# A mixture-of-experts stage in a fused two-layer block: biases, router and first matmuls rearranged

## The chip, the cores and the metric

The kernel runs on one core of one Trainium2 chip. The metric is the device time of one execution in microseconds (us); lower is better. Engines: PE is TensorE, DVE VectorE, ACT ScalarE, POOL GpSimd, SP SyncE, which here only issues DMAs.

## What is computed

Two layers over 2048 tokens of width 128 (8 sequences of 256). Layer 0 is an adaptive layer norm with causal attention (16 heads of 8), a second adaptive layer norm, and a feed-forward of nine experts: eight chosen by a router (two for each token, weights renormalised) and one shared. Layer 1 is a gated recurrence with a small MLP and a second mixture of eight experts. The change touches the feed-forward of layer 0:

```python
def _ffn(x, w1, b1, w2, b2):
    h = jax.nn.gelu(x @ w1.T + b1)
    return h @ w2.T + b2
logits = xf @ router_w.T + router_b
routing = softmax(logits)
sel_w, sel_idx = top_k(routing, 2)
sel_w = sel_w / sel_w.sum(-1)
comb[token, sel_idx] = sel_w
out = _ffn(xf, shared...) + sum_e comb[:, e] * _ffn(xf, spec_e...)
```

## The kernel before, in words

Activations lie transposed: 128 features on the partitions, tokens along the free axis, in four blocks of 512 tokens (t = 0 to 3). X is the residual stream, HN the normalised input. Matrix products keep fp32 precision by splitting each operand into a rounded upper part and a rest (HH and HL of the input, WH and WL of the weights, GH and GL of the hidden layer) and adding three matmuls (`three`, lines 1125 to 1129).

Each engine has its own instruction list, written out by hand in the order of execution, with waits on semaphores between them. The list around the change, in the order of the program:

The **end of attention** (lines 854 to 916 on VectorE, 1285 to 1350 on TensorE): units of one head group at a time, then the out projection (`out_proj`, four matmuls of 512 columns), and the second layer norm, called norm 1: `mean`, `centre`, `square`, `variance`, `inverse` (Ln and Exp on ScalarE), `normalise`, `split_hidden` (GpSimd, HH) and `rest` (VectorE, HL). Blocks 0 to 2 of it run early; block 3 comes last, since it waits for the last sequence's attention.

The **router** (`router`, line 1156; `route`, line 699): 16 tiny matmuls make logits in PSUM for all tokens. VectorE adds the router's bias, takes a maximum and subtracts it, ScalarE takes one Exp (`router_exp`), and 15 small VectorE instructions, each waiting for the one before, find the largest and the second largest (a tie goes to the lower expert), and divide. COMB then has a share for each token and expert, with 1 for the shared one. TensorE transposes it (`route_out`), VectorE copies the nine rows to CT (line 923), SyncE stores them in memory and loads each row back, repeated on all 128 partitions, as WB (lines 224 to 234).

The **experts**, one step for each of 36 pairs m of expert and block. TensorE computes four hidden chunks of 128 (`hidden0`, chunk c of step m+1) alternating with four output chunks of step m (`output0`). ScalarE takes Gelu twice from PSUM, into G and rounded into GH (lines 508 and 509); VectorE subtracts (`lower0`, line 937) to give GL; `output0` waits for GL. VectorE multiplies the finished output by WB (`moe_scale`, line 756), and GpSimd adds it to ACC (line 312) and splits the weights two experts ahead (lines 289 and 292). One step has 24 matmuls of 512 columns on TensorE.

How the first steps differ: `lower0` of step 0 is done by GpSimd (line 349), which splits expert 1's weights after it. ACC starts as the sum of the output biases: four matmuls of B2 with CT in full fp32 (`bias_out`, line 1361, one after each output chunk of step 1) and four VectorE copies (`bias_sum`, line 928).

## Time and profile before

| what | value |
|---|---|
| median of 3 runs | 679.75 us (679.01 to 680.6) |
| the profiled execution | 679.79 us, of which the span from first to last instruction is 678.0 us |
| PE, DVE, ACT, POOL busy | 606.8, 545.4, 486.1, 173.3 us |
| mean granted TensorE clock | 0.949 of 2.4 GHz |
| the chain that ended last, by engine | PE 62%, DVE 26%, ACT 5%, issue 5% |
| the expert stage of layer 0 | from about 214 to 430 us of the span |

Busy shares are means over stages that are bound by different things. What a change in one stage is worth is read from that stage: which engine is never idle there, and for what the others wait. The chain that ended last follows the work back from the last instruction. The granted clock is 1.00 at 2.4 GHz and 0.50 at 1.2 GHz.

### The profile page before, as it was taken

Reading aid. Unit: us, or ns where it says so; the run is one execution under the profiler, and the core shown is the slowest. Engines: PE = TensorE matmul, PEld = TensorE weight load, DVE = VectorE, ACT = ScalarE, POOL = GpSimd, SP = SyncE. Lnnn points to the kernel's source line nnn. Section 1 sums busy time; section 2 is a strip of 40 time slices with the busy share of each in tenths; the row PEclk is TensorE's granted clock in tenths of the full one; section 3 lists DMA queues with packets and bytes.
Section 4 is the critical chain, followed back from the end, with each engine's and each line's share of the span. In section 5 each row is a group of like instructions: output and inputs, shape, how many; then the busy total and the mean of one; then the engine's idle time right before and its main releaser. Section 6 shows DMA issues by size and latency. Waiting matters only on the chain.

```text
span 678.0 us, 11084 instructions
## 1 busy us (share of the span) xinstructions
PE 606.8 (89%) x3284; PEld 441.1 (65%) x3284; DVE 545.4 (80%) x1345; ACT 486.1 (72%) x857; POOL 173.3 (26%) x147
## 2 busy tenths in 40 slices
PE   8788889888997899999999999782699899999996
PEld 5355556555545568888888887351385788888884
DVE  3667888888866658878888887756899689999997
ACT  4548999999553669999999998677635466666663
POOL 3422223332301415443554443310143000000000
PEclk9789999999996899999999999976699799999999
DMA  7000000000100120122202220000000042222201
GB/s 239 1 0 2 2 2 0 0 0 0 32 1 0 48 113 37 57 95 94 91 2 93 93 85 1 23 1 0 0 1 0 1 150 87 87 86 86 86 1 62
DMA packets 6651, 29.85 MB, mean 44 GB/s; under 512 B 887, under 2 KB 1024, under 8 KB 4417
## 3 DMA queue, kind: packets, MB, share of 16 engines
q1 hardware_dynamic: 6610, 29.37, 12.2%
q8 instruction: 18, 0.29, 0.2%
q14 instruction: 23, 0.19, 0.1%
HBM read 28.18 MB, written 1.19 MB: 43 GB/s over the span
## 4 chain that ended last, share of the span: by engine, by line
PE 62%; DVE 26%; issue 5%; ACT 5%; DMA 1%; SPq 0%; POOL 0%; DVEq 0%; ACTq 0%; POOLq 0%
PE PS L1127 16%; PE PS L1129 16%; PE PS L1128 16%; DVE STAT L802 8%; PE PS L1273 2%; DVE RA L822 2%; PE PS L1228 2%; DVE HN L656 2%; PE PS L1153 2%; DMA AR<-in_wmod 1%; DVE SU L828 1%; PE PS L1242 1%; DVE HN L652 1%; ACT RA L605 1%; DVE AR L1086 1%
## 5 line engine op out<-in xcount | busy, mean ns | idle before, releaser
L937 DVE TENSOR_TENSOR RA<-AR,RA 128x512 fp32r<-128x512 f32 x140 | 134.3, 983 | 29.1 <-ACT RA L509 28.4
L508 ACT ACTIVATE AR<-PS,BI 128x512 f32<-128x512 f32 x144 | 99.4, 691 | 26.2 <-PE PS L1129 16.6
L1127 PE MATMUL PS<-HH,WH 128*128 128x512 f32 x272 | 109.5, 403 | 0.1
L1129 PE MATMUL PS<-HL,WH 128*128 128x512 f32 x272 | 107.4, 395 | 0.0
L1128 PE MATMUL PS<-HH,WL 128*128 128x512 f32 x272 | 107.3, 395 | 0.0
L509 ACT ACTIVATE RA<-PS,BI 128x512 fp32r<-128x512 f32 x144 | 98.4, 683 | 0.0
L802 DVE CUSTOM_DVE_ANT_0 STAT<-PS,MQ 128x128 f32<-128x128 f32 (+1 forms) x256 | 76.3, 354 | 20.2 <-PE PS L1229 20.1
L1127 PE MATMUL PS<-RA,WH 128*128 128x512 f32 x208 | 82.4, 396 | 2.5 <-DVE RA L1093 2.1
L1129 PE MATMUL PS<-RA,WH 128*128 128x512 f32 x208 | 81.2, 391 | 0.0
L1128 PE MATMUL PS<-RA,WL 128*128 128x512 f32 x208 | 81.2, 390 | 0.0
L312 POOL TENSOR_TENSOR AR<-AR 128x512 f32<-128x512 f32 x32 | 51.2, 1601 | 111.9 <-DVE AR L756 111.9
L335 POOL TENSOR_TENSOR RA<-QKT,RA 128x512 fp32r<-128x512 f32 x32 | 40.8, 1275 | 110.5 <-ACT RA L437 107.5
L605 ACT ACTIVATE RA<-AR 128x512 fp32r<-128x512 f32 x64 | 40.4, 632 | 34.2 <-DVE AR L1086 33.3
L1127 PEld LDWEIGHTS PS<-HH,WH 128*128 128x128 f32 x272 | 52.2, 192 | 15.6 <-ACT RA L509 3.0
L1129 PEld LDWEIGHTS PS<-HL,WH 128*128 128x128 f32 x272 | 51.9, 191 | 11.1
L1128 PEld LDWEIGHTS PS<-HH,WL 128*128 128x128 f32 x272 | 52.2, 192 | 10.7 <-issue 0.2
L444 ACT ACTIVATE AR<-PS 128x768 f32<-128x768 f32 x64 | 48.4, 808 | 13.7 <-PE PS L1246 11.6
L1153 PE MATMUL PS<-STAT,OND 128*128 128x512 f32 x48 | 31.5, 762 | 22.6 <-ACT STAT L386 22.6
L1093 DVE TENSOR_TENSOR RA<-AR,RA 128x512 fp32r<-128x512 f32 x64 | 44.3, 691 | 7.5 <-ACT RA L605 2.7
L599 ACT ACTIVATE AR<-PS 128x512 f32<-128x512 f32 x64 | 38.2, 597 | 13.8 <-PE PS L1129 11.8
L1127 PEld LDWEIGHTS PS<-RA,WH 128*128 128x128 f32 x208 | 39.2, 188 | 12.5 <-DVE RA L1093 3.2
L1086 DVE TENSOR_TENSOR AR<-AR 128x512 f32<-128x512 f32 x64 | 43.8, 685 | 2.2 <-ACT AR L614 2.2
(196 smaller groups left out, 1185.1 us busy)
## 6 DMA issues: line engine op xcount, KB each, us to landing
AR<-comb SPq DMA_DIRECT2D x16, 1024.0 KB, 4.6
WS<-in_w SPq DMA_DIRECT2D x9, 512.0 KB, 5.6
WS<-in_w SPq DMA_DIRECT2D x8, 384.0 KB, 3.1
M<-in_mats SPq DMA_DIRECT2D x1, 1384.0 KB, 12.2
X<-in_xT SPq DMA_DIRECT2D x4, 256.0 KB, 4.8
out_xT<-X SPq DMA_DIRECT2D x4, 256.0 KB, 2.1
AR<-in_wmod SPq DMA_DIRECT2D x1, 768.0 KB, 9.2
KM<-in_kmats SPq DMA_DIRECT2D x1, 162.5 KB
```

The source lines that it names most:

```text
L312: gp.tensor_tensor(out=blk(ACC, t), in0=blk(ACC, t), in1=YW[:, t % 2, :], op=ALU.add)\
L444: act.activation(PR[:, n0 % 2, 2 * h:2 * h + 2, :], PS[:, 2 + 2 * h:4 + 2 * h, 0:384], ACT.Exp, scale=SCALE).then_inc(exp_done, 1)
L508: act.activation(G[:, c, :], PS[:, c, :], ACT.Gelu_apprx_tanh, bias=bias).then_inc(s["act"], 1)
L509: act.activation(GH[:, m0 % 2, c, :], PS[:, c, :], ACT.Gelu_apprx_tanh, bias=bias)\
L605: act.activation(GH[:, m % 2, c, :], G[:, c, :], ACT.Copy).then_inc(s1["gh"], 1)
L802: mm = dve.tensor_tensor_reduce(out=MASKED_S[:, q, j, 0:width], in0=PS[:, j, first:first + width], in1=MQ[:, 256 - width:256], scale=-1.0, ...
L937: dve.tensor_tensor(out=GL[:, m0 % 2, c, :], in0=G[:, c, :], in1=f(GH[:, m0 % 2, c, :]), op=ALU.subtract).then_inc(s["lo"], 1)
L1086: dve.tensor_tensor(out=G[:, c, :], in0=G[:, c, :], in1=WB[:, e % 2, t * BLK:(t + 1) * BLK], op=ALU.mult).then_inc(s1["ymul"], 1)
L1127: pe.matmul(out, wh, xh, start=first, stop=False)
L1128: pe.matmul(out, wl, xh, start=False, stop=False)
L1129: return pe.matmul(out, wh, xl, start=False, stop=last)
L1153: pe.matmul(PS[:, variance_bank(k, t), :], OND[:, :], blk(STAT, t), start=True, stop=True)\
```

## The change

Five edits in the feed-forward of layer 0. The output biases are no longer summed by matmuls: a column `b2` for each expert joins the vectors, `moe_scale` adds it in the same VectorE instruction that multiplies by WB, and GpSimd fills ACC with the shared expert's bias. The routing no longer needs the softmax: two are chosen from the logits, and the shares are (1 ± tanh((second − first)/2))/2, the tanh being a ScalarE instruction between two Gelus. The small routing instructions stand between those of `lower0` of step 0, which VectorE now does. The hidden chunks of step 0 stand ahead of the last block's variance and normalisation on TensorE, and expert 1's weights are split ahead of the norm on GpSimd. The transposes stand in step 1 where they stood in step 0, and the VectorE loop over 24 steps is written out.

GpSimd:

```diff
             gp.wait_ge(moe[0]["w_in"], 16)
             split_weights(0, 0, 0, 1024)
+            gp.wait_ge(moe[0]["w_in"], 32)
+            split_weights(0, 1, 1, 1024)
             for t in range(NBLK):
                 split_hidden(1, HN, t)
-            for c in range(4):
-                gp.wait_ge(moe[0]["act"], 2 * (c + 1))
-                gp.tensor_tensor(out=GL[:, 0, c, :], in0=G[:, c, :], in1=f(GH[:, 0, c, :]), op=ALU.subtract)\
-                  .then_inc(moe[0]["lo"], 1)
-            gp.wait_ge(moe[0]["w_in"], 32)
-            split_weights(0, 1, 1, 1024)
+            gp.wait_ge(wo_done, 4)
+            shared_bias = V[:, VAT["b2"] + E0 - 1:VAT["b2"] + E0]
+            gp.tensor_scalar(ACC, shared_bias.to_broadcast([128, TOK]), 1.0, 0.0, ALU.mult, ALU.add)\
+              .then_inc(moe[0]["acc_init"], 1)
```

ScalarE:

```diff
-            router_exp(0)
...
+            def router_tanh():
+                act.wait_ge(s["odds"], 1)
+                act.activation(ODDS[:, :], RM["den"][:, :], ACT.Tanh, scale=0.5).then_inc(s["exps"], 1)
...
-            for m in range(8):
+            gelus(0, 0, 0)
+            gelus(1, 1, 0, between=router_tanh)
+            for m in range(2, 8):
                 gelus(m, m, m // 4)
```

VectorE, first `moe_scale`, then the list:

```diff
-                dve.tensor_tensor(out=YW[:, m0 % 2, :], in0=PS[:, 4 + m0 % 4, :],
-                                  in1=WB[:, slot, t * BLK:(t + 1) * BLK], op=ALU.mult).then_inc(s["ymul"], 1)
+                dve.scalar_tensor_tensor(out=YW[:, m0 % 2, :], in0=PS[:, 4 + m0 % 4, :], scalar=bias,
+                                         in1=WB[:, slot, t * BLK:(t + 1) * BLK], op0=ALU.add, op1=ALU.mult)\
+                   .then_inc(s["ymul"], 1)
...
+            centre(1, 3)
             rest(1, HN, 0)
             rest(1, HN, 1)
-            centre(1, 3)
             rest(1, HN, 2)
             normalise(1, 3)
             rest(1, HN, 3)
-            route(0, E0)
...
-            dve.wait_ge(s["lo"], 4)
-            lower0(1, 1)
-            for t in range(NBLK):
-                bias_sum(t)
+            lower0(0, 0, (largest, first_equal, second_largest, second_chosen))
+            shares()
+            lower0(1, 1, (nothing, nothing, first_rows_in, last_rows_in))
             lower0(2, 2)
```

TensorE:

```diff
             router(0, 0)
             router(0, 1)
             mean(1, 3)
             router(0, 2)
+            pe.wait_ge(s["split"], 2)
+            hidden0(0, 0, 0)
+            hidden0(0, 0, 1)
             variance(1, 3)
+            hidden0(0, 0, 2)
+            hidden0(0, 0, 3)
             router(0, 3)
...
-            for c in range(4):
-                hidden0(0, 0, c)
-            step0(0, 0, 1, between=routes_between)
-            step0(1, 1, 1, between=biases_between)
+            step0(0, 0, 1)
+            step0(1, 1, 1, between=routes_between)
```

`largest`, `first_equal`, `second_largest`, `second_chosen` and `shares` hold 2, 3, 5, 3 and 5 small instructions. `first_rows_in` and `last_rows_in` are the copies of line 923, two each.

The first place is TensorE's list from the last block's mean (`X,OND`) to the first expert matmul. M,HN is a router matmul, STAT,OND the variance, HH and HL with WH and WL a hidden chunk. Before:

```order
L1140 MATMUL PS<-X,OND 128x512 [waits x_upd]
L1161 MATMUL PS<-M,HN 128x8 [waits hn_done]
L1161 MATMUL PS<-M,HN 128x8 x3
L1153 MATMUL PS<-STAT,OND 128x512 [waits lnv_done,sq_done]
L1161 MATMUL PS<-M,HN 128x8 [waits hn_done]
L1161 MATMUL PS<-M,HN 128x8 x3
L1127 MATMUL PS<-HH,WH 128x512 [waits moe0_split,hl_done]
```

Now:

```order
L1195 MATMUL PS<-X,OND 128x512 [waits x_upd]
L1216 MATMUL PS<-M,HN 128x8 [waits hn_done]
L1216 MATMUL PS<-M,HN 128x8 x3
L1182 MATMUL PS<-HH,WH 128x512 [waits cen_done,hl_done,moe0_split]
L1183 MATMUL PS<-HH,WL 128x512
L1184 MATMUL PS<-HL,WH 128x512
L1182 MATMUL PS<-HH,WH 128x512 [waits cen_done,hl_done]
...
L1208 MATMUL PS<-STAT,OND 128x512 [waits lnv_done,sq_done]
L1182 MATMUL PS<-HH,WH 128x512 [waits cen_done,hl_done]
...
L1216 MATMUL PS<-M,HN 128x8 [waits hn_done]
```

Two hidden chunks now stand ahead of the last variance and two behind it, and the last router matmuls follow them.

The second place is VectorE's list from the last `rest` to the second subtraction of step 1 (RA<-AR,RA is `lower0`). Now:

```order
L675 TENSOR_TENSOR HL<-HN,HH 128x512 [waits hh_done]
L751 MEMSET COMB 128x16
L754 TENSOR_TENSOR AR<-PS,ROWS 128x128 [waits moe0_logits,in_rows]
L757 TENSOR_REDUCE RM_m<-AR 128x16 [waits moe0_rstep]
L1001 TENSOR_TENSOR RA<-AR,RA 128x512 [waits moe0_act]
L762 TENSOR_TENSOR AR<-AR,RM_m 128x128 [waits moe0_rstep]
...
L797 TENSOR_TENSOR AR<-AR,ODDS 128x128 [waits moe0_exps,moe0_rstep]
L799 TENSOR_TENSOR AR<-AR 128x128 [waits moe0_rstep]
L801 TENSOR_SCALAR COMB<-AR 128x16x8 [waits moe0_rstep]
L1001 TENSOR_TENSOR RA<-AR,RA 128x512 [waits moe0_act] x2
L981 COPY AR<-PS 9x512 [waits moe0_combT] x2
```

Before, all the routing (19 instructions) and its four copies stood ahead of the first subtraction on this engine.

The third place is GpSimd's list around the hidden split. Before:

```order
L289 TENSOR_SCALAR WH<-WS 128x1024 [waits moe0_w_in]
L292 TENSOR_TENSOR WL<-WS,WH 128x1024 [waits moe0_split]
L300 TENSOR_SCALAR HH<-HN 128x512 [waits hn_done] x4
L349 TENSOR_TENSOR RA<-AR,RA 128x512 [waits moe0_act] x4
```

Now:

```order
L291 TENSOR_TENSOR WL<-WS,WH 128x1024 [waits moe0_split]
L288 TENSOR_SCALAR WH<-WS 128x1024 [waits moe0_w_in]
...
L299 TENSOR_SCALAR HH<-HN 128x512 [waits hn_done] x4
L350 TENSOR_SCALAR AR<-V 128x2048 [waits wo_done]
```

The second weight split stands ahead of the hidden split, and the fill of ACC (2048 columns) directly behind its last block.

## Rows read from the trace of the kernel before

**Rows 1.** Stretches: us, PE, PEld, DVE, ACT, POOL busy (count), PE clock, DMA.

```profile
215.00:220.00 5.00, 5.00 (x14) 4.05 (x15) 3.73 (x13) 3.15 (x6) 0.12 (x1) 0.50 0.00 0
...
300.00:400.00 100.00, 100.00 (x443) 82.84 (x442) 86.06 (x93) 92.93 (x153) 50.46 (x29) 1.00 0.18 64
```

**Rows 2.** The chain that ended last, 190 to 262 us: start, us, what.

```profile
215.78 0.30 DVE AR L721
...
230.25 0.92 PE PS L1174 x8
...
233.91 1.05 PE PS L1366 x2
...
244.24 0.50 PE PS L1127
```

**Rows 3.** The timeline, end of the norm to the first Gelu: start, us, engine.

```profile
206.68 1.28 DVE L668 TENSOR_TENSOR HL<-HN,HH 128x512 fp32r<-128x512 f32 x2
...
209.28 1.65 PE L1153 MATMUL PS<-STAT,OND 128*128 128x512 f32 x2 [1.40 <-ACT STAT L386]
210.97 0.69 ACT L392 ACTIVATE STAT<-PS,CON 128x512 f32<-128x512 f32 x1 [1.74 <-PE PS L1153]
...
213.08 0.73 DVE L656 TENSOR_SCALAR HN<-HN,MC,MOD 128x256 f32<-128x256 f32 x2
...
214.55 0.69 DVE L668 TENSOR_TENSOR HL<-HN,HH 128x512 fp32r<-128x512 f32 x1 [0.74 <-POOL HH L300]
...
217.24 1.28 ACT L508 ACT_TABLE_LOAD   x1
```

**Rows 4.** The timeline, routing on VectorE beside GpSimd.

```profile
219.88 5.16 POOL L349 TENSOR_TENSOR RA<-AR,RA 128x512 fp32r<-128x512 f32 x4 [5.37 <-ACT RA L509]
...
220.02 0.29 DVE L738 TENSOR_REDUCE RM_km<-AR 128x16 f32<-128x128 f32 x1
...
220.34 0.98 DVE L739 TENSOR_TENSOR AR<-AR,RM_km 128x128 f32<-128x128 f32 x1
...
225.01 1.04 POOL L289 TENSOR_SCALAR WH<-WS 128x1024 fp32r<-128x1024 f32 x1
```

**Rows 5.** The timeline near the end of attention.

```profile
175.80 2.35 POOL L292 TENSOR_TENSOR WL<-WS,WH 128x1024 fp32r<-128x1024 f32 x1
175.86 2.32 DVE L815 TENSOR_TENSOR MP<-NM,MP 128x8 f32<-128x8 f32 x1
...
178.18 0.33 SPq L223 DMA_DIRECT2D WS<-in_w  x1
...
183.77 0.17 DVE L815 TENSOR_TENSOR MP<-NM,MP 128x8 f32<-128x8 f32 x1
...
184.23 0.43 DVE L828 STREAM_SHUFFLE SU<-OT 128x256 f32<-128x256 f32 x1
...
186.11 0.42 DVE L822 TENSOR_TENSOR RA<-RA,PS 128x256 fp32r<-128x256 f32 x1 [1.44 <-PE PS L1282]
```

**Rows 6.** DMA issues between 170 and 200 us, with us to landing.

```profile
WS<-in_w SPq DMA_DIRECT2D x1, 512.0 KB, 4.6
```

**Rows 7.** Groups, 260 to 420 us: line, count | busy, mean ns | idle before, releaser.

```profile
L937 DVE TENSOR_TENSOR RA<-AR,RA 128x512 fp32r<-128x512 f32 x118 | 119.1, 1033 | 24.7 <-ACT RA L509 24.1
```

**Rows 8.** Views of single lines: ns min/median/max, first and last start.

```profile
L756 DVE TENSOR_TENSOR AR<-PS,AR x32: 676/683/684, 250.6 to 419.2; 128x512 f32<-128x512 f32 x32
...
L1031 DVE SCALAR_TENSOR_TENSOR AR<-PS,V,AR x12: 735/743/750, 490.7 to 509.4; 128x512 f32<-128x512 f32 x12
```

**Rows 9.** The gates' way through memory: issues, landing, first use.

```profile
232.08 0.31 SPq L225 DMA_DIRECT2D comb<-AR  x1
234.53 0.82 SPq L228 DMA_DIRECT2D AR<-comb  x2
...
DMA to landing us min/median/max: 4.3/4.5/6.5
...
250.56 0.68 DVE L756 TENSOR_TENSOR AR<-PS,AR 128x512 f32<-128x512 f32 x1
```

More of the change, by code:

```diff
@@ L30, with build @@
 MAT_AT, MN = columns(MATS)
[L33 removed]
+def build(nc, xT, wmod, vecs, mats, kmats, rows, w0, w1, comb0, comb1, outT):
     f32, r32, bf16 = mybir.dt.float32, mybir.dt.float32r, mybir.dt.bfloat16
@@ L510, in gelus @@
                        .then_inc(s["act"], 1)
+                    if between and c == 1:
+                        between()
                     if m0 % 4 == 3 and c == 0 and m0 < 35:
@@ new lines, in _, with each, route1, link @@
+            lg, e, k1, k2, e2, w = (RT[k][:, :, :] for k in ("lg", "e", "k1", "k2", "e2", "w"))
+            peak, m1, km1, m2, km2, den = (RM[k][:, :] for k in ("m", "m1", "km1", "m2", "km2", "den"))
+            prio = V[:, VAT["prio"]:VAT["prio"] + 8].unsqueeze(1).to_broadcast([128, 16, 8])
+            logits = PS[:, 7, 0:128].rearrange("p (i e) -> p i e", e=8)
+            def each(x):
+                return x.unsqueeze(2).to_broadcast([128, 16, 8])
+            def route1():
+                s = moe[1]
+                count = [0]
+                def link(ins):
+                    count[0] += 1
+                    ins.then_inc(s["rstep"], 1)
+                    dve.wait_ge(s["rstep"], count[0])
+                dve.wait_ge(s["logits"], 1)
+                dve.tensor_copy(lg, logits).then_inc(s["lg"], 1)
@@ L744, in route, with largest @@
                 dve.tensor_tensor(out=COMB[:, :, 0:8], in0=w, in1=each(den), op=ALU.mult).then_inc(s["comb"], 1)
-                if ne == 9:
-                    dve.memset(COMB[:, :, 8:9], 1.0).then_inc(s["comb"], 1)
-            def moe_scale(s, m, m0, pair):
+            def largest():
+                s = moe[0]
+                dve.memset(COMB[:, :, 8:9], 1.0).then_inc(s["comb"], 1)
+                dve.wait_ge(in_rows, 16)
+                dve.wait_ge(s["logits"], 1)
+                dve.tensor_tensor(out=lg, in0=logits, in1=ROWS[:, 128:136].unsqueeze(1).to_broadcast([128, 16, 8]),
+                                  op=ALU.add).then_inc(s["rstep"], 1)
+                dve.wait_ge(s["rstep"], 1)
+                dve.tensor_reduce(m1, lg, axis=AX.X, op=ALU.max).then_inc(s["rstep"], 1)
@@ new lines, in first_equal, with second_largest @@
+            def first_equal():
+                s = moe[0]
+                dve.wait_ge(s["rstep"], 2)
+                dve.tensor_tensor(out=k1, in0=lg, in1=each(m1), op=ALU.is_equal).then_inc(s["rstep"], 1)
+                dve.wait_ge(s["rstep"], 3)
+                dve.tensor_tensor(out=k1, in0=k1, in1=prio, op=ALU.mult).then_inc(s["rstep"], 1)
+                dve.wait_ge(s["rstep"], 4)
+                dve.tensor_reduce(km1, k1, axis=AX.X, op=ALU.max).then_inc(s["rstep"], 1)
+            def second_largest():
+                s = moe[0]
+                dve.wait_ge(s["rstep"], 5)
+                dve.tensor_tensor(out=k1, in0=k1, in1=each(km1), op=ALU.is_equal).then_inc(s["rstep"], 1)
+                dve.wait_ge(s["rstep"], 6)
+                dve.scalar_tensor_tensor(out=e2, in0=k1, scalar=-3e38, in1=lg, op0=ALU.mult, op1=ALU.add)\
+                   .then_inc(s["rstep"], 1)
+                dve.wait_ge(s["rstep"], 7)
+                dve.tensor_reduce(m2, e2, axis=AX.X, op=ALU.max).then_inc(s["rstep"], 1)
+                dve.wait_ge(s["rstep"], 8)
+                dve.tensor_tensor(out=den, in0=m2, in1=m1, op=ALU.subtract).then_inc(s["odds"], 1)
+                dve.tensor_tensor(out=k2, in0=e2, in1=each(m2), op=ALU.is_equal).then_inc(s["rstep"], 1)
@@ new lines, in second_chosen, with shares @@
+            def second_chosen():
+                s = moe[0]
+                dve.wait_ge(s["rstep"], 9)
+                dve.tensor_tensor(out=k2, in0=k2, in1=prio, op=ALU.mult).then_inc(s["rstep"], 1)
+                dve.wait_ge(s["rstep"], 10)
+                dve.tensor_reduce(km2, k2, axis=AX.X, op=ALU.max).then_inc(s["rstep"], 1)
+                dve.wait_ge(s["rstep"], 11)
+                dve.tensor_tensor(out=k2, in0=k2, in1=each(km2), op=ALU.is_equal).then_inc(s["rstep"], 1)
+            def shares():
+                s = moe[0]
+                dve.wait_ge(s["rstep"], 12)
+                dve.tensor_tensor(out=e, in0=k2, in1=k1, op=ALU.subtract).then_inc(s["rstep"], 1)
+                dve.tensor_tensor(out=w, in0=k1, in1=k2, op=ALU.add).then_inc(s["rstep"], 1)
+                dve.wait_ge(s["rstep"], 14)
+                dve.wait_ge(s["exps"], 1)
+                dve.tensor_tensor(out=e, in0=e, in1=each(ODDS[:, :]), op=ALU.mult).then_inc(s["rstep"], 1)
+                dve.wait_ge(s["rstep"], 15)
+                dve.tensor_tensor(out=w, in0=w, in1=e, op=ALU.add).then_inc(s["rstep"], 1)
+                dve.wait_ge(s["rstep"], 16)
+                dve.tensor_scalar(COMB[:, :, 0:8], w, 0.5, None, ALU.mult).then_inc(s["comb"], 1)
@@ L750, in moe_scale @@
+            def moe_scale(s, m, m0):
+                bias = V[:, VAT["b2"] + m // 4:VAT["b2"] + m // 4 + 1]
+                pair = m // 8
                 slot = m0 // 4 % 2
```

107 lines of the change are left out of this document (39 added, 68 removed).

## The prediction

> **What bounds the kernel now.** I read the stretches first. From 300 to 400 us, in the middle of the expert stage, TensorE is busy all the time at the full clock, 443 matmuls in 100 us, 0.226 us each, so a step of 24 takes 5.44 us; ScalarE's 153 instructions take 0.61 us each and leave it free for 7% of the time [rows 1]. VectorE has idle time there too: 24.7 us ahead of 118 subtractions, 0.84 us for each step of four [rows 7]. So nothing off TensorE can speed up the middle, and what can be won lies in the opening. From 215 to 220 us the clock is at its lower level, 1.2 GHz [rows 1]. Then the chain that ended last: the logits are ready at 215.78, and only at 244.24 does TensorE take up step 2 and is never idle again until the stage ends [rows 2]. Between lie 48 matmuls of steps 0 and 1 and 12 of the first hidden chunks; at 0.226 us all 60 are 13.6 us of work in 28.5 us. The chain there goes through routing on VectorE, transposes and four full-precision bias matmuls of 1.05 us each [rows 2]. The timeline gives the norm ahead of it [rows 3], and shows VectorE held up by GpSimd in two places [rows 4, 5]. The mark to follow is **the start of step 2**, 244.24 us: whatever it gains, the kernel gains, since the stage behind it is bound by TensorE.
>
> **The change part by part.** All times are those of the profiled execution, 679.79 us with a span of 678.0; the median of the three runs, 679.75, is the same to 0.04.
>
> *End of attention, +0.95 us.* The split of expert 1's weights moves here, and its load is issued at 178.18 [rows 5] and lands 4.6 us later [rows 6], at 182.8. GpSimd then rounds for 1.04 us [rows 4] and subtracts for 2.35, which for expert 0 held a VectorE instruction of 0.17 us for 2.32 [rows 5]. The same instruction (line 815) comes next at 183.77, when the rounding is about to end (183.85). I expect the subtraction to hold it until 186.3. Behind it stand a divide and a shuffle, over 0.73 us after its own end [rows 5], so line 822, for which TensorE waits, starts at 187.05 in place of 186.11. Bounds: 0, if the hold misses it; 2.3, the whole hold on the path. I take 0.95, by the rows' own times. TensorE's out projection covers the rest of the hold.
>
> *The norm of block 3, -0.4 us.* On VectorE `centre` now precedes the three `rest` of 0.64 us [rows 3]. First `rest` done: 206.7 + 0.65 + 0.65 = 208.1, when TensorE takes the first hidden chunk, where it was idle before. Two chunks, 6 x 0.226 = 1.36, then the variance at 209.5. It took 1.65 us until 210.97 at the lower clock [rows 3]; two passes of that size take 1.05 at the upper one [rows 2], which I expect, as TensorE is no longer idle just before. So ScalarE reads it at 210.57 and the norm ends at 213.4 instead of 213.81 [rows 3]. The other two hidden chunks fill a stretch in which TensorE was idle. Bound: +0.8 with the low clock. The order of `centre` and `rest` and the early wait for the split (long done at 186.3) cost nothing.
>
> *The first subtraction, -2.9 us.* It ended at 221.2 on GpSimd (219.88 plus a quarter of 5.16) [rows 4]. Now: logits 1.95 us after the norm as before (213.81 to 215.78 [rows 2, 3]), at 215.35. GpSimd's HH of block 3 is ready 0.74 us after the norm [rows 3], at 214.15, and the fill of ACC follows at once. The trace has no such fill; 1024 columns took 1.04 us [rows 4], so 2048 take about 2.1, to 216.2. Its input is one column read over and over. Whether that holds VectorE is not shown. The upper bound is the whole 2.1 us: beside GpSimd's subtraction, a routing instruction with two operands in SBUF took 0.98 in place of 0.29, while a one-operand reduce kept its 0.29 [rows 4]. The lower bound is 0. I take the whole hold, as the `rest` of block 3, also with two such operands, is released at the very moment: it runs from 216.2 to 216.9, the two instructions of `largest` at a pitch of 0.32 [rows 4] to 217.5, the subtraction of 0.69 to 218.2. Without the hold the logits decide: 215.35 + 0.64 + 0.69 = 216.7.
>
> The Trainium skill (SBUF — State Buffer, Who interferes with whom) says that a VectorE instruction with two SBUF inputs contends with a GpSimd one that reads SBUF, not with one that only writes. By it the fill, which reads its column, would hold, and the result is the 669.1 below; counted as a mere write it would be 667.6.
>
> ScalarE is no limit: the Exp is gone, and the table load of 1.28 us [rows 3] moves behind the norm's last Exp (about 211.9), so Gelus run from 213.5, two of them 1.3 us by the mean of rows 1, far ahead of 217.5.
>
> *From there to step 2.* VectorE: 3, 5 and 3 small instructions between subtractions, then 5 for the shares, 16 x 0.32 = 5.1; three more subtractions of step 0 and the first of step 1, 4 x 0.65 = 2.6. That is 7.7 us. TensorE then still has four output and three hidden chunks of 0.68 and 2 x 0.92 of transposes [rows 2]: 6.6. Together 14.35. TensorE's own work from the first output chunk on is 45 matmuls and the transposes, 10.2 + 1.8 = 12.0; I expect the low clock for its first 4 us, as after idle time in rows 1, which adds 2: also 14. So step 2 starts at 218.2 + 14.3 = 232.5, and the opening gains 244.24 - 232.5 = **11.7 us**. The copies, 0.65 each, and the bias matmuls and copies that are gone, 4 x 1.05 on TensorE, lie within this count. The tanh is a small instruction ready before its Gelu is.
>
> *The middle, 0.* `moe_scale` becomes a three-operand instruction; one with the same operands (line 1031) has 743 ns, `moe_scale` 683 [rows 8]. 0.06 us a step against 0.84 idle: hidden. If that idle time were gone, 32 steps would cost 2. At the stage's end, where VectorE finishes, one is on the path: +0.1 with rounding. The written-out loop adds no instruction and I cost it at 0.
>
> *The gates.* The last copy ended at about 232.0, the store was issued at 232.08, the first row's load at 234.53, landing in 4.5 us (4.3 to 6.5), about 7 after the store; the first use was at 250.56, 6.3 after step 2's start [rows 2, 9]. Now the copies end at about 230.7, so the gates land near 237.7 to 239.7 and are wanted at 238.8: late by 0.9 at most. Queued behind the scale is the next step's subtraction, which TensorE wants a step (5.44 us) later, so this costs nothing. It was covered by 11 us before, and is not now.
>
> Sum: 0.95 - 11.7 + 0.1 = -10.65, and 679.79 - 10.65 = **669.1 us**.
>
> **The rivals.**
> 1. *Neither hold bites.* The fill lets VectorE through and the split misses line 815. 1.5 and 0.95 less: 666.7. For it: the fill has a one-column input, and a landing 0.3 us off changes who is first. Against it: both holds are in the trace [rows 4, 5].
> 2. *The clock stays low through the opening.* The 45 matmuls at 0.45 us and slower transposes make 23.1 us of the 14.3, and the time 677.9; a clock that comes back 6 us later than I take costs 3, 672.1. For it: TensorE still pauses three times between the hidden chunks and the first output. Against it: once TensorE was kept busy before, the clock rose in the opening itself, and the two transposes-of-eight at 0.92 are at the upper level [rows 2].
> 3. *The gates come late.* Beyond about 4 us of lateness VectorE, and so TensorE, waits. With the longest landing, 6.5, and the next weights ahead of it, 1 to 2 us: 670.6.
> 4. *VectorE becomes the bound and the kernel is slower.* The place is `moe_scale`, if its third operand made it wait for GpSimd. It decides from 0.84 - 0.06 + 10.65/32 = 1.1 us more a step. If it waited for one whole GpSimd subtraction of 5.16/4 = 1.29 [rows 4] and the next expert's rounding of 1.04 each time, 2.3 a step, 32 x (2.3 - 0.78) = 49 less 10.65 gives 718; at 1.29 alone, 32 x 0.51 = 16 less 10.65, **685.4**. Against it: the present one never took more than 684 ns, the three-operand one never over 750 [rows 8].
> 5. *The change doesn't do what it says: a second table load.* Two loads of 1.28 us around the tanh, one of them hidden: 670.4. The changed instruction list has none there. The Trainium skill (ScalarE: Activation LUTs, Table sets: the hidden batching unit) lists tanh with exp and with sigmoid, not with gelu, by which such loads would be needed.
>
> **How the numbers follow.** My forecast has 0.62 and its own range, 667.6 to 671, from the bounds of fill, split and clock; rival 1 has 0.18, rival 2 0.09, rival 3 0.06, rival 4 0.04, rival 5 0.01. The range 666.2 to 672.1 takes in rivals 1, 3, 5 and the milder half of 2. A measurement of this kernel tells about 0.2%, 1.4 us, from no change. Faster by more: all but rival 4 and the end of rival 2, 0.95; within: 0.01; slower 0.04.
>
> **What would show it.** Step 2 starts near 233.5 (232.5 and the 0.95) instead of 244.2. Line 815's second-last instance lasts over 2 us. The fill takes about 2.1 us, and the `rest` of block 3 or the first subtraction ends late by it. The steps from 260 to 400 stay at 5.44 us with TensorE always busy. The scale's mean is near 743 ns. No table load stands between the first Gelu and the end of the stage. The prediction is wrong if step 2 starts outside 230 to 237, or if TensorE shows idle time behind it.

## The result, and the profile after

The changed kernel takes **672.12 us** (median of 4 runs, 668.48 to 673.97), beside 680.17 for the kernel before on the same chip (4 runs, 679.01 to 681.92): a ratio of 0.9899, 95% interval 0.987 to 0.9929. The medians differ by 8.05 us; the ratio, which is not their quotient (0.988), stands for 6.9 us, and where kernels of different groups are compared below, I go by the ratios. The forecast was 669.1, faster by 10.65 us, with a range of 666.2 to 672.1, so the time lies at the slow edge, 0.02 us outside. The profiled execution is the slowest of the four: 673.97 us, span 672.2.

Its stretches, in the columns of [rows 1]:

```profile
190.00:200.00 10.00, 10.00 (x63) 4.47 (x56) 4.75 (x13) 3.96 (x9) 0.00 (x0) 0.83 0.00 0
...
210.00:215.00 5.00, 4.71 (x16) 3.44 (x15) 3.42 (x7) 0.63 (x1) 0.62 (x1) 0.64 0.00 0
215.00:220.00 5.00, 4.08 (x10) 2.20 (x8) 1.38 (x3) 2.70 (x4) 0.00 (x0) 0.68 0.00 0
...
300.00:400.00 100.00, 100.00 (x443) 82.78 (x442) 87.87 (x94) 93.03 (x153) 47.65 (x28) 1.00 0.21 78
```

The middle is untouched: 443 matmuls in 100 us, as in [rows 1]. VectorE, which has the longer scale, is still off the limit. Groups of 260 to 420 us, and the view of the scale's line and the tanh's:

```profile
L1001 DVE TENSOR_TENSOR RA<-AR,RA 128x512 fp32r<-128x512 f32 x117 | 117.1, 1026 | 21.4 <-ACT RA L512 20.1
```

```profile
L813 DVE SCALAR_TENSOR_TENSOR AR<-PS,V,AR x32: 735/743/746, 245.2 to 413.9; 128x512 f32<-128x512 f32 x32
...
L499 ACT ACTIVATE ODDS<-RM_den x1: 217/217/217, 228.5 to 228.5; 128x16 f32<-128x16 f32 x1
```

The idle time ahead of the subtractions is 21.4 us in place of the 24.7 of [rows 7], and the scale is 743 ns, exactly the row of line 1031 in [rows 8]. What failed lies ahead of all this. First, the timeline near the end of attention (start, us, engine), which answers to [rows 5]:

```profile
183.91 3.60 PE L1328 MATMUL PS<-AR,M 128*128 128x512 f32 x8
...
184.71 1.04 POOL L288 TENSOR_SCALAR WH<-WS 128x1024 fp32r<-128x1024 f32 x1 [4.92 <-DMA WS<-in_w]
...
185.20 0.58 DVE L871 CAST MP<-NM 128x8 fp32r<-128x8 f32 x1
...
185.82 0.17 DVE L873 TENSOR_TENSOR MP<-NM,MP 128x8 f32<-128x8 f32 x1
185.84 2.36 POOL L291 TENSOR_TENSOR WL<-WS,WH 128x1024 fp32r<-128x1024 f32 x1
185.93 2.56 DVE L894 TENSOR_TENSOR AR<-OT,SU 128x256 f32<-128x256 f32 x1
...
188.75 0.41 DVE L880 TENSOR_TENSOR RA<-RA,PS 128x256 fp32r<-128x256 f32 x1
...
189.30 0.64 PE L1313 MATMUL PS<-AR 128*32 128x256 f32 x8 [1.58 <-DVE RA L880]
```

Line 873 (line 815 before) starts 0.02 us ahead of GpSimd's subtraction and gets away; the divide behind it (line 894) is held in its place, 2.56 us, and TensorE stands idle for 1.58 us. Then the norm of block 3, which answers to [rows 3]:

```profile
211.07 1.62 PE L1216 MATMUL PS<-M,HN 128*128 128x8 f32 x8 [0.29 <-DVE HN L663]
...
212.54 0.77 PE L1182 MATMUL PS<-HH,WH 128*128 128x512 f32 x1
...
214.82 0.63 PE L1184 MATMUL PS<-HL,WH 128*128 128x512 f32 x1
...
215.25 1.91 PE L1208 MATMUL PS<-STAT,OND 128*128 128x512 f32 x2
...
217.20 0.69 ACT L391 ACTIVATE STAT<-PS,CON 128x512 f32<-128x512 f32 x1 [4.92 <-PE PS L1208]
...
218.72 1.28 ACT L511 ACT_TABLE_LOAD   x1
...
220.71 1.90 POOL L350 TENSOR_SCALAR AR<-V 128x2048 f32<-128x2048 f32 x1
220.78 2.36 DVE L675 TENSOR_TENSOR HL<-HN,HH 128x512 fp32r<-128x512 f32 x1 [0.74 <-POOL HH L299]
...
223.59 0.68 DVE L1001 TENSOR_TENSOR RA<-AR,RA 128x512 fp32r<-128x512 f32 x1
```

Six matmuls of the hidden chunks stand ahead of the variance and take 2.7 us (212.54 to 215.25), and ScalarE has waited 4.92 us when it reads the variance, against 1.74 in [rows 3]. The fill (1.90) holds the last `rest` for 2.36.

To find where time went I cut each profiled execution at six marks: the start of the subtraction of expert 0's weights (175.80 in [rows 5]), `centre` of block 2, `centre` of block 3, the end of block 3's `normalise` (its two line-663 instructions included), the end of the first `lower0` instruction of step 0, the first `moe_scale` (250.56 in [rows 9]), and the end of the span. The start of output in step 2, which the prediction calls "the start of step 2", is less sharp: step 2's first hidden chunk runs ahead of it. The first scale is the better mark. By the prediction's own mark it missed as well: step 2's first output matmul starts at 239.06, where it had 233.5 and called itself wrong outside 230 to 237.

```profile
239.06 0.39 PE L1182 MATMUL PS<-RA,WH 128*128 128x512 f32 x1
```

The parts of each row add up to its span.

| | to split | to centre 2 | to centre 3 | norm | to first lower | to first scale | to end | span |
|---|---|---|---|---|---|---|---|---|
| before | 175.80 | 22.00 | 10.08 | 5.93 | 7.36 | 29.39 | 427.43 | 678.0 |
| forecast | 175.80 | 22.95 | 15.61 for both | | 4.8 | 20.7 | 427.5 | 667.4 |
| changed | 177.45 | 24.61 | 8.88 | 9.10 | 4.23 | 20.98 | 426.91 | 672.2 |

The first part is the same code in both kernels, but for one small load at the very start. In the 13 profiled executions of this study with some change it lies between 173.3 and 177.45 us, so 1.65 of the changed kernel's excess there is scatter, as its median shows too. The real misses are the second part, +1.66 against the forecast, and the third and fourth together, 17.98 in place of 15.61, +2.37. The fifth came out 0.57 better, the last 0.6 better, the sixth 0.3 worse.

### The profile page after: what moved, and what is told of

The parts are those of the page before. It is cut to its first block, busy times and chain, and to the rows that moved or that the text cites. A ratio compares the mean times of both kernels' runs of the same rounds, so it can differ in the third digit from the quotient of the medians.

```text
span 672.2 us, 10961 instructions
## 1 busy us (share of the span) xinstructions
PE 605.4 (90%) x3276; PEld 444.0 (66%) x3276; DVE 546.4 (81%) x1344; ACT 485.9 (72%) x857; POOL 167.2 (25%) x144
## 4 chain that ended last, share of the span: by engine, by line
PE 62%; DVE 25%; ACT 6%; issue 5%; DMA 1%; POOL 0%; DVEq 0%; SPq 0%; ACTq 0%; POOLq 0%
PE PS L1182 16%; PE PS L1184 16%; PE PS L1183 16%; DVE STAT L860 9%; PE PS L1328 2%; PE PS L1195 2%; DVE RA L880 2%; PE PS L1283 2%; PE PS L1208 2%; DVE SU L886 1%; ACT AR L554 1%; PE PS L1297 1%; ACT RA L612 1%; DVE AR L1141 1%; DVE RA L1148 1%
## 5 line engine op out<-in xcount | busy, mean ns | idle before, releaser
L1001 DVE TENSOR_TENSOR RA<-AR,RA 128x512 fp32r<-128x512 f32 x144 | 138.2, 983 | 27.1 <-ACT RA L512 25.7
L1148 DVE TENSOR_TENSOR RA<-AR,RA 128x512 fp32r<-128x512 f32 x64 | 44.2, 690 | 8.1 <-ACT RA L612 3.3
L1208 PE MATMUL PS<-STAT,OND 128*128 128x512 f32 x48 | 29.6, 721 | 21.2 <-ACT STAT L385 21.2
L1131 DVE TENSOR_TENSOR AR<-PS,AR 128x512 f32<-128x512 f32 x64 | 43.8, 684 | 2.2 <-ACT AR L606 2.1
```

What stands on the lines that cost most here:

```text
L1001: dve.tensor_tensor(out=GL[:, m0 % 2, c, :], in0=G[:, c, :], in1=f(GH[:, m0 % 2, c, :]), op=ALU.subtract).then_inc(s["lo"], 1)
L1131: dve.tensor_tensor(out=G[:, c, :], in0=PS[:, 2 + c, :], in1=SG[:, c, :], op=ALU.mult)\
L1148: dve.tensor_tensor(out=GL[:, m % 2, c, :], in0=G[:, c, :], in1=f(GH[:, m % 2, c, :]), op=ALU.subtract).then_inc(s1["lo"], 1)
```

## The experiments

All timed runs were made in three groups of four; the kernels of one group ran on one chip beside the kernel before. The columns of the table above, for all of them, stand at the end of this section.

### The changed kernel again, and one hold or wait taken away at a time

The first group asks what each of the three suspects is worth: the early weight split, the fill, and the hidden chunks ahead of the variance. The control is the changed kernel, unedited (`changed, again` in the table).

> The changed kernel again, beside three variants of it. Both theories: 668 to 674 us, median near 671.5. Theory A (the lower clock of TensorE costs the missing gain, brought on by two edits: the early split holds VectorE near the end of attention, and the hidden chunks stand ahead of the variance while the clock is low): the out projection behind the hold takes 4.9 us in place of 3.6 in the profile again, and the last variance 1.9 us. Theory B (the missing gain is chance: an early stretch, 30 to 50 us, ran at a lower clock in that one execution): these two are at 3.6 and 1.0 to 1.7 us here, and the time is nearer to 669.

It took 671.99 us (6 runs, 671.52 to 673.22) beside 678.25 of before: ratio 0.9908, 0.9885 to 0.9931. All parts are those of the first profile within 0.2 us but for the scatter ahead of the first mark. The out projection behind the hold takes 4.95 us and the last variance 1.91, as theory A had it.

**Expert 1's split late.**

```diff
-            gp.wait_ge(moe[0]["w_in"], 32)
-            split_weights(0, 1, 1, 1024)
-            for t in range(NBLK):
+            for t in range(3):
                 split_hidden(1, HN, t)
+            gp.wait_ge(hl_done, 3)
+            gp.wait_ge(moe[0]["w_in"], 32)
+            split_weights(0, 1, 1, 1024)
+            split_hidden(1, HN, 3)
```

> Expert 1's weights are split behind the third rest, while VectorE is idle for 5 us. Theory A: no VectorE instruction of over 2 us at the end of attention beyond the one that the kernel before has, the out projection back at 3.6 us, and 2.6 us off the changed kernel (1.0 for the hold, 1.6 for the clock). If only the hold counts: 1.0. Theory B: under 0.5 us.

669.65 us (6 runs), ratio 0.9877 (0.9852 to 0.9903). The second part is back at 22.00, as before the change: the early split alone had made it 24.5. By the ratios the edit is worth 2.1 us of the 2.6 expected. The norm is 7.45, and its timeline shows that the split found another victim.

```profile
209.04 1.02 PE L1210 MATMUL PS<-STAT,OND 128*128 128x512 f32 x2
...
209.90 2.38 POOL L291 TENSOR_TENSOR WL<-WS,WH 128x1024 fp32r<-128x1024 f32 x1
...
211.48 1.35 DVE L661 TENSOR_TENSOR HN<-XC,STAT 128x512 f32<-128x512 f32 x1 [2.79 <-ACT STAT L395]
```

The normalisation takes 1.35 us in place of 0.69. TensorE was at its upper level here (granted clock 1.00 from 205 to 215 us), so the variance took 1.02; less the 0.66 of the hold, the norm is 6.8 by my estimate.

**ACC filled by ScalarE.**

```diff
-            gp.wait_ge(wo_done, 4)
-            shared_bias = V[:, VAT["b2"] + E0 - 1:VAT["b2"] + E0]
-            gp.tensor_scalar(ACC, shared_bias.to_broadcast([128, TOK]), 1.0, 0.0, ALU.mult, ALU.add)\
-              .then_inc(moe[0]["acc_init"], 1)
...
             square(1, XC, 3)
+            act.wait_ge(wo_done, 4)
+            shared_bias = V[:, VAT["b2"] + E0 - 1:VAT["b2"] + E0]
+            act.activation(ACC, shared_bias.to_broadcast([128, TOK]), ACT.Copy).then_inc(moe[0]["acc_init"], 1)
             inverse(1, 3)
```

> ACC is filled by ScalarE while it waits for the last variance. As predicted, the fill on GpSimd holds VectorE for 1.9 us: without it the last rest is 0.69 us in place of 2.36, and the logits decide, so 1.2 to 1.7 us off. If the fill's hold was hidden anyway: 0. ScalarE's fill (about 1.9 us) must be over before the variance is; if not, it costs up to 1.

668.3 us (6 runs), ratio 0.9851 (0.9825 to 0.9878). The last `rest` lasts 0.69 and the fifth part is 2.56 in place of 4.22: the hold cost **1.67 us**. The median fell by more, 3.7 us; in the profiled execution the load of expert 1's weights landed early and the divide went free (second part 22.50), which is not the edit's doing. ScalarE's fill lies in a wait that was there anyway:

```profile
208.31 1.89 ACT L489 ACTIVATE AR<-V 128x2048 f32<-128x2048 f32 x1
...
213.18 0.69 ACT L387 ACTIVATE STAT<-PS,CON 128x512 f32<-128x512 f32 x1 [2.97 <-PE PS L1207]
...
216.76 0.69 DVE L674 TENSOR_TENSOR HL<-HN,HH 128x512 fp32r<-128x512 f32 x1 [0.74 <-POOL HH L299]
```

**The variance ahead of the hidden chunks.**

```diff
             router(0, 2)
+            variance(1, 3)
             pe.wait_ge(s["split"], 2)
             hidden0(0, 0, 0)
             hidden0(0, 0, 1)
-            variance(1, 3)
             hidden0(0, 0, 2)
```

> The last variance stands ahead of all four hidden chunks. Theory A: ScalarE reads it about 3.2 us earlier, the norm ends 3.2 us earlier, the hidden chunks then delay the last router matmuls, and 2.0 to 2.9 us come off. Theory B (the place of the chunks is harmless, a high clock would have kept the norm at the forecast -0.4): 0 to 0.7 us off.

666.05 us (6 runs, 664.56 to 670.84), ratio 0.9835 (0.98 to 0.987). The norm takes 6.37 in place of 9.06, **2.7 us less**, though the variance itself ran at the lower level (2.07 us). In this execution the load of expert 1's weights also landed so early that the split missed the divide (second part 22.02), which is chance and not the edit.

### The combination, the old position, and the bias edit alone

**All three edits together**, and the same with `router(0, 3)` between hidden chunks 1 and 2.

> The three edits of the first job together: late split, fill by ScalarE, variance ahead of the hidden chunks. Added up by the segments of their profiles (2.5 for the hold and the clock behind it, 1.7 for the fill, 2.7 for the norm) 6.9 us off the changed kernel's 672.0: 665.1. If the 5.9 that the variance alone gave over its 2.7 was more than chance, 662. If the split placed in VectorE's idle time now meets its subtractions, since the norm ends earlier: 667.

> As b_best, with the last router matmuls after two of the four hidden chunks. With the fill gone the logits decide the first subtraction; they come 1.3 us earlier at the upper clock and 2.6 at the lower: 1 to 2 us less than b_best if that is so, the same if TensorE's work decides by then.

The first took 666.26 us (5 runs, ratio 0.9816, 0.9787 to 0.9844), the second 667.68 (5 runs, 0.9844, 0.9822 to 0.9866). Neither is what the three gains would sum to (665.1), and the second, expected level with the first or 1 to 2 us below it, came out 1.4 above it. In both, the norm is 7.4 again. With the variance earlier, the normalisation comes earlier too, and meets the late split in full:

```profile
210.08 2.39 POOL L291 TENSOR_TENSOR WL<-WS,WH 128x1024 fp32r<-128x1024 f32 x1
210.76 2.26 DVE L660 TENSOR_TENSOR HN<-XC,STAT 128x512 f32<-128x512 f32 x1 [1.89 <-ACT STAT L391]
```

So moving a hold is not removing it; the late split and the earlier variance undid part of each other. There is a second such clash. With the variance early, ScalarE's fill is no longer over in time, and the Ln that reads the variance waits behind it. The same place in the last combination below, where nothing else holds the norm:

```profile
208.10 1.90 ACT L495 ACTIVATE AR<-V 128x2048 f32<-128x2048 f32 x1
...
208.25 1.12 PE L1213 MATMUL PS<-STAT,OND 128*128 128x512 f32 x2 [0.20 <-ACT STAT L387]
...
209.90 0.67 ACT L393 ACTIVATE STAT<-PS,CON 128x512 f32<-128x512 f32 x1
```

The variance is done at 209.37 and read at 209.90: 0.5 us on the path, in all three kernels that have both edits.

**The hidden chunks back behind all of the norm** (variance, then the last router matmuls, then the four chunks; the rest as changed).

```diff
             router(0, 2)
+            variance(1, 3)
+            router(0, 3)
             pe.wait_ge(s["split"], 2)
             hidden0(0, 0, 0)
             hidden0(0, 0, 1)
-            variance(1, 3)
             hidden0(0, 0, 2)
             hidden0(0, 0, 3)
-            router(0, 3)
```

> The changed kernel with the four hidden chunks behind the last router matmuls, as before the change. Theory A (hoisting the chunks pays, only their place ahead of the variance costs): the norm ends as early as in a_var, but the chunks, 2.7 to 5.1 us, lie on the path to the first output: 3 us above a_var, 669 to 670. Rival (the fill's hold covers the chunks, so hoisting gains nothing): the same as a_var, 666.

669.92 us (6 runs), ratio 0.9899 (0.987 to 0.9928), as theory A had it. The norm is 6.34, as with the variance first; but the fifth part is 5.44 in place of 4.22. Chunks behind the variance and ahead of the last router matmuls are worth that 1.2 us, since their Gelus then run during the norm; chunks ahead of the variance lose 2.7. The change had both.

**The bias edit alone, on the kernel before:** the `b2` column, the three-operand scale, no bias matmuls or copies, the fill behind the second split, the loop written out; the attention, norm, router and routing lists are those of before.

```diff
-            step0(1, 1, 1, between=biases_between)
+            step0(1, 1, 1)
...
-                dve.tensor_tensor(out=YW[:, m0 % 2, :], in0=PS[:, 4 + m0 % 4, :],
-                                  in1=WB[:, slot, t * BLK:(t + 1) * BLK], op=ALU.mult).then_inc(s["ymul"], 1)
+                dve.scalar_tensor_tensor(out=YW[:, m0 % 2, :], in0=PS[:, 4 + m0 % 4, :], scalar=bias,
+                                         in1=WB[:, slot, t * BLK:(t + 1) * BLK], op0=ALU.add, op1=ALU.mult)\
+                   .then_inc(s["ymul"], 1)
```

> The kernel before with the bias edit alone: no bias matmuls and copies, the bias added in the scale instruction, ACC filled by GpSimd behind the second weight split, the scale loop written out. Step 1 took 12.3 us in the chain of before (231.2 to 243.5) in place of 5.4, so 6.5 us off the kernel before: 671.7. If the gates, whose cover shrinks by as much, came late, 4. If the three-operand scale slowed the middle, up to 2 less gain.

671.44 us (6 runs, 668.92 to 673.78) beside 677.54: ratio 0.9908, 0.9881 to 0.9935, **the same as the whole change**, and as expected (671.7). Its sixth part is 21.95 against 29.39. The chains of before and of this kernel show what went:

```profile
226.28 1.41 PE PS L1174 x8
...
230.25 0.92 PE PS L1174 x8
...
236.54 1.05 PE PS L1366 x2
237.59 0.43 PE PS L1127
238.02 0.24 PE PS L1128
...
243.51 0.69 DVE RA L937
```

```profile
226.86 1.04 PE PS L1170 x8
...
229.29 0.87 PE PS L1170 x8
230.16 0.23 PE PS L1123
...
242.89 0.23 PE PS L1125
243.12 0.23 PE PS L1123
```

Each of the four bias matmuls was 1.05 us on the path, 4.2 together, and the first matmul behind each took 0.43 in place of 0.23. From the first transposes to the first scale it was 24.28 us (226.28 to 250.56) and is 16.84 (226.86 to 243.70), 7.44 less. But 1.5 of that is not the edit: from the first to the second transposes the code is the same, and it took 3.97 us in the execution of before, whose six matmuls there ran at 0.43 us each, and 2.43 here, at 0.23. The clock had come back earlier. From the second transposes on it was 20.31 us and is 14.41: **5.9 us** for the bias edit, close to the 6.1 of the medians.

### The hold cut in pieces, and the rest

**GpSimd's subtraction for expert 1 in four instructions of 256 columns**, at its early place, nothing else.

```diff
+                if isinstance(e, int) and n == 0 and e == 1:
+                    for q in range(0, 1024, 256):
+                        ins = gp.tensor_tensor(out=WL[:, 1, q:q + 256], in0=WS[:, q:q + 256],
+                                               in1=f(WH[:, 1, q:q + 256]), op=ALU.subtract)
+                    ins.then_inc(s["split"], 1)
+                    return
```

> The changed kernel with one edit: GpSimd's subtraction for expert 1 is issued as four instructions of 256 columns, at the same place. Theory: the 2.4 us loss ahead of block 2's centre is one whole GpSimd instruction for which a VectorE instruction with two SBUF inputs has to wait, so the longest piece, about 0.6 us, is all it can wait at a time. From the start of expert 0's split to the centre of block 2: 22.0 to 22.9 us instead of 24.4; time 1.5 to 2.4 us below the changed kernel, 669.6 to 670.5. Rival: GpSimd keeps the access for its whole run of instructions, or each piece is waited for in turn: 24.4 us again and 672.

The timeline has the same meeting of the same two instructions as in the changed kernel, and the divide now waits for one piece:

```profile
185.20 0.17 DVE L879 TENSOR_TENSOR MP<-NM,MP 128x8 f32<-128x8 f32 x1
185.22 2.98 POOL L293 TENSOR_TENSOR WL<-WS,WH 128x256 fp32r<-128x256 f32 x4
185.31 0.94 DVE L900 TENSOR_TENSOR AR<-OT,SU 128x256 f32<-128x256 f32 x1
...
187.32 0.42 DVE L886 TENSOR_TENSOR RA<-RA,PS 128x256 fp32r<-128x256 f32 x1 [0.71 <-PE PS L1343]
```

0.94 in place of 2.56, TensorE decides again when line 886 starts, and the second part is 22.00. The norm, in this execution at the upper level with the chunks still ahead of the variance, takes 6.80:

```profile
209.31 0.47 PE L1188 MATMUL PS<-HH,WH 128*128 128x512 f32 x1 [0.23 <-issue]
...
210.55 0.40 PE L1190 MATMUL PS<-HL,WH 128*128 128x512 f32 x1
210.78 1.02 PE L1214 MATMUL PS<-STAT,OND 128*128 128x512 f32 x2
...
211.84 0.69 ACT L397 ACTIVATE STAT<-PS,CON 128x512 f32<-128x512 f32 x1 [2.61 <-PE PS L1214]
```

The median is 670.59 us (5 runs), ratio 0.9898 (0.9878 to 0.9917) against 0.9908 for the changed kernel in its own group: 0.7 us lower by the ratios, less than either interval can tell, where 1.5 to 2.4 was expected. The mechanism is shown in the profile; a gain of this edit by itself in the time is not. Its profiled execution lost against the control's 1.6 us ahead of the first mark, 0.7 in the sixth part and 1.2 behind the first scale, in code that is the same.

**The three causes removed, with no new hold of VectorE:** the pieces, ScalarE's fill, and the variance first. The diffs are those above.

> The changed kernel with three edits: the subtraction of expert 1 in four pieces at its early place, the fill of ACC by ScalarE, and block 3's variance ahead of all hidden chunks. Theory: the three losses lie one behind the other and add: 1.5 to 2.4 (hold at the end of attention) + 2.7 (norm) + 1.7 (fill) = 5.9 to 6.8 below the changed kernel, so 665.2 to 666.1 with the changed kernel at 672; stretch from the centre of block 3 to the end of the norm 6.4 us, from there to the end of the first subtraction 2.6 us. Rival: the work that follows takes part of it back, as in the combination with the late split (first subtraction to first scale 21.97 us instead of 21.0): 666.5 to 667.5.

**663.06 us** (5 runs, 660.54 to 664.37) beside 677.07 of before: ratio 0.9779, 0.9757 to 0.9801. Between 180 and 240 us VectorE waits for no more than one piece at a time, `rest` and normalisation are not held, and TensorE is at its upper level throughout:

```profile
180.00:240.00 60.00, 56.29 (x292) 36.22 (x288) 44.38 (x107) 42.24 (x73) 8.20 (x10) 1.00 0.14 52
```

The same stretch of the changed kernel had 258 matmuls at a granted clock of 0.86. The expectation was 5.9 to 6.8 us below the changed kernel; by the ratios it is 8.7. Part of the excess is the clock: the norm is 5.87 in place of the 6.4 expected, although 0.5 of it is the wait behind ScalarE's fill shown above. In the first combination the clock was 0.58 from 215 to 220 us, and its sixth part is 21.97; here it is 20.29.

**The variance first, once more.**

> The kernel with only block 3's variance ahead of the hidden chunks, once more, on another chip run. Theory: the order of TensorE's work is worth 2.7 us (9.06 to 6.37 from the centre of block 3 to the end of the norm), and the other 3 us of the first measurement (666.05) came from a load that happened to land early and so let the split miss the divide: if it lands late, 669.3 and 24.4 us ahead of block 2's centre; if early, 667 and 22.0. Rival: the order itself is worth the 5.9 us: 666 with the split held.

667.45 us (4 runs, 666.75 to 669.28), ratio 0.985 (0.9831 to 0.9869), beside 0.9835 the first time, so the edit's time repeats. In this execution the divide was held (second part 24.66), and the norm took 6.55. The time lies between the two expectations for a held divide, 669.3 and 666. By the ratios the edit gives 4 to 5 us over the changed kernel (0.9908 less 0.985 and 0.9835, times 678). The norm accounts for 2.5 to 2.7 of it and the part up to the first scale for 0.3 to 0.7 (20.69 and 20.29 against 21.01). What remains is 0.7 to 2 us; in the first measurement's profile the missed divide would more than cover it, in the second I can't place it.

**No output biases at all, the loop kept.** This kernel leaves the output biases of layer 0's experts out of the result.

> The kernel before with the second layer's biases of the first expert stage left out altogether: no bias matmuls, no copies to ACC (GpSimd sets it to 0), moe_scale and its loop as they are. Leaves out: the spec and shared b2 of layer 0. It splits what the bias edit gave (671.4, -6.1 against before on its chip). Theory: all of it is the four bias matmuls and copies on the path, so this run gives the same, 671 to 672, first subtraction to first scale 21.5 to 22.5 us instead of 29.4. Rival: some of it came from the written-out loop or the later stage: then 672.5 to 674.

671.83 us (6 runs, 670.09 to 675.98), ratio 0.9922 (0.9895 to 0.9949). With neither the three-operand scale nor the written-out loop it gains as much as the bias edit within the intervals. Its sixth part, 23.24, misses the expected 21.5 to 22.5, but ahead of the second transposes: there the lower clock lasted longer, with 1.88 us for the first eight transposes. From the second transposes on it is 14.42 us (230.58 to 245.00), beside 14.41 with the bias edit. So the gain is the missing matmuls and copies, and the other two edits cost nothing that shows.

### All cuts in one table

The granted clock of the norm is told by the duration of the variance: 1.02 to 1.13 us at the upper level, 1.9 to 2.1 at the lower. The 1.65 us of before lies between: there the level changed on the way.

| | ratio | to split | to centre 2 | to centre 3 | norm | to first lower | to first scale | to end |
|---|---|---|---|---|---|---|---|---|
| changed, again | 0.9908 | 175.40 | 24.45 | 8.88 | 9.06 | 4.22 | 21.01 | 427.0 |
| split late | 0.9877 | 175.29 | 22.00 | 8.87 | 7.45 | 4.23 | 21.22 | 426.6 |
| ScalarE fills | 0.9851 | 175.70 | 22.50 | 8.86 | 8.96 | 2.56 | 20.31 | 426.6 |
| variance first | 0.9835 | 173.30 | 22.02 | 8.87 | 6.37 | 4.22 | 20.69 | 427.9 |
| the three | 0.9816 | 175.44 | 22.03 | 8.87 | 7.45 | 2.56 | 21.97 | 428.1 |
| the three, router moved | 0.9844 | 176.59 | 22.00 | 8.87 | 7.41 | 3.25 | 21.20 | 428.5 |
| chunks late | 0.9899 | 175.95 | 23.06 | 8.87 | 6.34 | 5.44 | 20.48 | 427.1 |
| bias edit alone | 0.9908 | 175.96 | 22.01 | 10.08 | 6.34 | 7.36 | 21.95 | 425.7 |
| split in pieces | 0.9898 | 177.02 | 22.00 | 8.87 | 6.80 | 4.23 | 21.72 | 428.2 |
| pieces, fill, variance | 0.9779 | 175.96 | 22.02 | 8.87 | 5.87 | 2.57 | 20.29 | 425.8 |
| variance first, again | 0.985 | 175.68 | 24.66 | 8.88 | 6.55 | 4.23 | 20.29 | 427.2 |
| no biases | 0.9922 | 175.98 | 22.00 | 10.07 | 6.35 | 7.36 | 23.24 | 428.5 |

## Why the prediction was right or wrong

**What bounds the kernel: right.** The middle did not move (443 matmuls in 100 us), and the change's gain came in the opening: behind the first scale the changed kernel takes 426.9 to 427.0 us against 427.43, within the scatter of that part (425.7 to 428.5).

**End of attention, forecast +0.95, measured +2.45 (24.45 against 22.00).** The hold itself was rightly sized. Where the clock stayed up (chunks late) the same 2.56 us hold cost 1.06, and all of it is line 880, for which TensorE waits: it starts 11.36 us behind the first mark (187.31) against 10.31 in before (186.11, [rows 5]). In the changed kernel's own profile it is 0.99 late, of 2.61. I had the wrong victim, the instruction ahead of the divide, and the right size. What failed is the sentence that TensorE's out projection covers the rest. I left out what TensorE did after its 1.58 us of idle time: from 190 to 200 us the granted clock was 0.83, and 0.89 in the control, against 1.00 before. There the next out projection took 4.95 us (in the control) in place of 3.60, and that is most of the other 1.6. Of the four profiled executions in which the divide was held, three show this lower clock and the fourth does not; of the ten others, none does. So the hold goes with it, but doesn't always bring it.

**The norm of block 3, forecast -0.4, measured +1.9 (8.88 + 9.06 against 10.08 + 5.93). This is the step that failed**, in its words "1.05 at the upper one, which I expect, as TensorE is no longer idle just before". TensorE was not idle: it was busy for 4.71 of the 5 us from 210 to 215, in the row at the top, and the clock was 0.64 all the same. `centre` ahead of the `rest` instructions came as allowed (206.7 is 8.9 behind block 2's): 8.88 for 10.08, a gain of 1.2 in every kernel that has it. With the upper clock the step comes out as I wrote it: the pieces' execution has 8.87 + 6.80 = 15.67, the forecast 15.61. But in the changed kernel the clock was at its lower level, and then everything ahead of the variance's reader grows, not the variance alone: the router's eight matmuls 1.62 for 1.06, six chunk matmuls 2.7 for 1.5, the variance 1.9 for 1.02. My bound for the lower clock, +0.8, is 1.2 us above the step's forecast, no more than the chunks' part alone (2.7 less 1.5). The order decides how much the clock can cost: chunks first 6.80 at the upper and 9.0 to 9.1 at the lower level, variance first 5.87 (with 0.5 of waiting for ScalarE's fill in it) and 6.34 to 6.55. The trace of before had rows that warned of it: the variance's 1.65 us in [rows 3], which I took for its price at the lower level and which is 1.9 to 2.1 there, and a granted clock of 0.50 from 215 to 220 us in [rows 1].

**First subtraction.** The fill was to take 2.1 us and hold for all of it, costing 1.5; it took 1.90 and cost 1.67. From the norm's end to the end of the subtraction I had 4.8, and it was 4.23: the mechanism is right and the size 0.6 too long; without the hold I had 3.3, and it was 2.56. By the Trainium skill's rule (SBUF — State Buffer, Who interferes with whom) a GpSimd instruction that reads SBUF contends; the trace agrees, with one column read over and over, 2.36 us for 0.69.

**From there to the first scale, forecast 20.7, measured 21.0 and 20.98:** right. I had given all of the opening's gain as one number; the bias edit alone shows its make-up. It gives 7.4 of it here, 5.9 by the removed matmuls and copies and 1.5 by the clock of that execution. By differences between single executions, the remaining edits gain 1.2 (`centre`), 3.1 (routing woven in, tanh, first subtraction on VectorE) and 0.9 here, and lose 2.45 and 2.7 in the two parts above: 5.2 against 5.15. That is why the whole change and the bias edit alone have the same ratio. None of these three gains was timed by itself, and which part of the 3.1 is the tanh and which the weaving isn't shown.

**The middle, the stage's end, the gates:** right. The scale is 743 ns and hidden. The last copy ended at 236.7, the loads were issued from 239.16 on, the first landed 4.8 us later, and the first scale started at 245.25 without a wait shown on it, so 1.3 us were in hand.

**The rivals.** Neither hold bites (666.7): both bit in the changed kernel; the split's can miss when its load lands early, as in one execution. The clock stays low (672.1 for the mild case): that its price is the measured time is luck, since I had placed it behind the first subtraction, where it cost nothing beyond the forecast (21.0 for 20.7), and not ahead of it. The mechanism, a lower clock, is the right one at another place. Late gates, VectorE as the bound and the second table load: none occurred. The tanh took 217 ns between two Gelus with no load, where the Trainium skill's table (ScalarE: Activation LUTs, Table sets: the hidden batching unit) would have led one to expect two.

What stays open is what decides whether the clock falls at these places. The changed kernel and the one with the chunks late differ only behind 200 us, and from 190 to 200 their clocks are 0.83 and 1.00; each profile is one execution.

## What to carry to other kernels

When work is hoisted ahead of a link of the critical chain on the same engine, price it at the lower clock, with every instruction that then stands ahead of that link; put it behind the link if the engine is idle there anyway. A long GpSimd instruction with its operands in SBUF is a hold looking for a victim: moving it only changes which VectorE instruction it meets, while cutting it into pieces shortens the hold to one piece, and giving it to ScalarE removes it, if ScalarE has the time free. And measure the simplest edit of a bundle alone: here it carried the whole gain, and the best version (0.9779) came from the others only when their three side effects were taken out.

## What the runs showed that I had not expected

- A VectorE instruction of one small input can be held as well: where the load landed at 181.75 (the kernel whose ACC ScalarE fills), `CAST MP<-NM` of 128x8 took 2.22 us beside GpSimd's subtraction, 0.17 alone. Beside GpSimd's rounding it took 0.40 to 0.63. In the first execution with the variance first, the subtraction (182.80 to 185.16) let an instruction with one operand in PSUM through untouched (line 880, 0.42 us, starting 0.8 us into it). The Trainium skill (SBUF — State Buffer, Who interferes with whom) counts casts among those that can take the shared access, and these rows agree.

```profile
183.30 2.35 POOL L291 TENSOR_TENSOR WL<-WS,WH 128x1024 fp32r<-128x1024 f32 x1
...
183.46 2.22 DVE L870 CAST MP<-NM 128x8 fp32r<-128x8 f32 x1
```

- Four pieces cost GpSimd 2.98 us in place of 2.36, and the divide got through behind the first.
- ScalarE fills 2048 columns from one column in 1.89 us, the time that GpSimd needs (1.90), and holds up nothing on VectorE; what it can delay is ScalarE's own next instruction.
- The part ahead of the first mark, with the same instructions on the compute engines everywhere, varied by 4.15 us between profiled executions (173.30 to 177.45). A single execution can't show a difference of 2 us in the whole; the cuts at marks could, though the clock reaches into them too, as by the 1.5 us between the transposes.
